# Two steps of expert tiles a round instead of three in the last rounds of a transformer kernel

## The reference

```python
x = x + _L0_xattn_ref(ctx_1024, _layernorm(x), mask, ...)     # 8 heads, keys from context and tokens
x = x + _L0_ffn_ref(_layernorm(x), weight_q, weight_scale, bias)   # int8 quantised 128x128 product
x = x + _L1_xattn_ref(_layernorm(x), ctx_1024, We, W2)        # softmax over the tokens
x = x + _L1_ffn_ref(_layernorm(x), Wr, br, W1, b1, W2, b2)    # 8 experts, argmax router
```

## Time and profile before

| | us |
|---|---|
| median of 3 runs | 1051.12 |
| lowest and highest | 1049.69, 1051.59 |
| the profiled execution | 1048.07 |
| its span in the trace | 1046.3 |
| mean granted TensorE clock in it | 0.986 |
| TensorE busy | 979.4 |
| VectorE busy | 795.1 |
| ScalarE busy | 740.3 |
| GpSimd busy | 468.0 |

### The profile page before, as it was taken

One profiled execution on the slowest core, in us unless ns is written; L12 is line 12 of the kernel. 1 busy time (PEld: TensorE's weight loads), 2 busy tenths in 40 slices (PEclk: granted clock), 3 DMA queues, 4 the chain that ended last, 5 costly groups with the idle time before them and its releaser, 6 DMA issues.

```text
span 1046.3 us, 31979 instructions
## 1 busy us (share of the span) xinstructions
PE 979.4 (94%) x10989; PEld 861.2 (82%) x10989; DVE 795.1 (76%) x2585; ACT 740.3 (71%) x1753; POOL 468.0 (45%) x1094
## 2 busy tenths in 40 slices
PE   2799999999999999999999999999998988887997
PEld 1688888888888888888888888888887878877897
DVE  3566778888888888888888888888888867755553
ACT  1688877777777777777777877777776655554564
POOL 3333323353545353535353535343434335664455
PEclk9999999999999999999999999999999998998999
DMA  5743000000000000000000000000000032011310
GB/s 133 213 115 61 3 2 2 2 12 2 12 1 10 0 10 0 10 0 10 0 10 0 10 3 8 3 7 5 5 7 6 5 70 74 30 34 50 87 50 22
DMA packets 45124, 28.38 MB, mean 27 GB/s; under 512 B 11039, under 2 KB 41698, under 8 KB 45042
## 3 DMA queue, kind: packets, MB, share of 16 engines
q1 hardware_dynamic: 39586, 17.79, 6.8%
q0 software_dynamic: 4320, 8.50, 2.5%
q10 hardware_dynamic: 1136, 1.05, 0.3%
HBM read 17.75 MB, written 10.02 MB: 27 GB/s over the span
## 4 chain that ended last, share of the span: by engine, by line
PE 80%; ACT 5%; DVE 4%; issue 4%; SPq 3%; POOL 2%; another core or an unknown queue 1%; DMA 1%; DVEq 0%; POOLq 0%; ACTq 0%
PE ps L1421 13%; PE ps L1384 10%; PE ps L1362 8%; PE ps L1188 7%; PE ps L1190 7%; PE ps L1189 7%; PE ps L1460 7%; PE ps L1349 4%; PE ps L1341 4%; PE ps L1446 3%; PE ps L1440 2%; SPq L399 2%; SPq L400 1%; PE ps L1216 1%; PE ps L1231 1%
## 5 line engine op out<-in xcount | busy, mean ns | idle before, releaser
L1080 DVE TENSOR_REDUCE sumsq<-qk_hat 128x8 f32<-128x512 f32 x192 | 124.0, 678 | 44.9 <-ACT qk_hat L491 44.6
L1421 PE MATMUL ps<-qT_all,kT_all 64*128 64x128 f32 x2048 | 149.6, 286 | 1.8 <-ACT w_all L500 1.2
L1384 PE MATMUL ps<-v_sb,prob 128*64 128x65 f32 x4096 | 144.5, 224 | 6.2 <-ACT qq_t L541 2.4
L1384 PEld LDWEIGHTS ps<-v_sb,prob 128*64 128x64 f32 x4096 | 129.0, 138 | 25.3 <-issue 13.3
L550 ACT ACTIVATE prob<-ps,neg_shift 128x512 f32<-128x512 f32 x128 | 88.6, 692 | 79.4 <-PE ps L1421 79.3
L1103 DVE TENSOR_TENSOR qk_hat<-ps,rstd 128x512 f32<-128x512 f32 x192 | 120.6, 684 | 26.9 <-POOL rstd L686 26.3
L491 ACT ACTIVATE qk_hat<-ps 128x512 f32<-128x512 f32 x192 | 113.3, 598 | 39.1 <-PE ps L1190 28.9
L1421 PEld LDWEIGHTS ps<-qT_all,kT_all 64*128 64x128 f32 x2048 | 125.0, 188 | 19.2 <-ACT prob L550 13.1
L1188 PE MATMUL ps<-w_hi,xc_hi 128*128 128x512 f32 x320 | 138.3, 432 | 0.8 <-DVE mask_bias L1155 0.8
L679 POOL TENSOR_TENSOR rs_t<-rs_y 128x32 f32<-128x32 f32 x73 | 17.8, 243 | 259.7 <-ACT rs_y L528 259.7
L1190 PE MATMUL ps<-w_hi,xc_lo 128*128 128x512 f32 x320 | 126.6, 396 | 0.0
(11 more groups left out here) (227 smaller groups left out, 2142.1 us busy)
## 6 DMA issues: line engine op xcount, KB each, us to landing
x_res<-sorted_rows SPq DMA_DIRECT2D x71, 65.5 KB
w_all<-in_L_ffn_W_dram SPq DMA_DIRECT2D x16, 256.0 KB, 5.9
x_res<-in_x_dram SPq DMA_DIRECT2D x5, 768.0 KB
ctx_res<-in_ctx_dram SPq DMA_DIRECT2D x5, 462.0 KB
out_dram<-o_n,x_res POOLq DMA_INDIRECT x71
sorted_rows<-stage,idx POOLq DMA_INDIRECT x64
sorted_rows<-fill SPq DMA_DIRECT2D x1, 524.0 KB, 5.2
sorted_rows<-table_fill SPq DMA_DIRECT2D x8, 65.5 KB
```

The source lines that it names most:

```text
L1080: nc.vector.reduce_sum(sumsq[:, n * H:(n + 1) * H], sq[:, n * INNER:(n + 1) * INNER].rearrange("p (h d) -> p h d", d=DH), AX).then_inc(ss_ ...
L1384: last = nc.tensor.matmul(dst[half:half + DH, :], prob[:, kt, at + half:at + half + DH], v_sb[:, 1 - par, kt, h, :], start=kt == 0, stop=k ...
L1421: last = nc.tensor.matmul(ps_s[2 * kt + half][:, cols], k_t[rows, kt, cols], q_t[rows, cols], start=True, stop=True)
```

## The change

Each of the rounds 64 to 74 takes two steps instead of three. The calls of place 1 go away on TensorE, ScalarE, VectorE and GpSimd; those of places 0 and 2 stay where they are in the order and take consecutive tiles. `tile_no` numbers them by `place // 2`. `REST`, the loop over the first list behind the last round, starts at step 21 instead of 32, so that 20 tiles of that list have their first product there, where it was 9. The table of the second list is still built in its first four steps. Number and order of the tiles, arithmetic and buffers are the same.

```diff
--- before.py
+++ after.py
@@ -327,7 +327,7 @@
         def one(res, b):
             return res[:, bass.ds(b, 1), 0:D].rearrange("p a d -> p (a d)")
 
-        TAIL, PLACES = B, 3
+        TAIL, PLACES = B, 2
         TOTAL_AT = 4 * (EARLY + 2) + 3
 
         def tail(j, inside):
@@ -335,7 +335,7 @@
 
         def tile_no(j, place):
 
-            return PLACES * (j - TAIL) + place - 1
+            return PLACES * (j - TAIL) + place // 2 - 1
 
         REST = range(PLACES * (LAST + 1 - TAIL) - 1, NA + 1)
         SECOND_PART = range(NA - 2, T + 1)
@@ -529,7 +529,6 @@
                                              bias=lift_bias[:, 0:1]).then_inc(y0_done, 1)
 
                 if tail(j, inside):
-                    tile(tile_no(j, 1), 0)
                     roots()
                 if rho == 0 and group(g - 1, inside):
 
@@ -703,7 +702,6 @@
                     nc.gpsimd.tensor_copy(mask_now[:, 1 - par:2 - par], mask_bias[:, bass.ds(j + 1, 1)]).then_inc(mask_set, 1)
 
                 if tail(j, inside):
-                    store(tile_no(j, 1), 0)
                     if g - 2 == NG - 1 and rho == 0:
                         scatter(g - 2, (0, 1), inside)
                     store(tile_no(j, 2), 0)
@@ -1065,10 +1063,8 @@
                 window(j, par, rho, g, inside)
                 if tail(j, inside):
                     finish(tile_no(j, 0), 0)
-                    prep(tile_no(j, 1), 0)
                     if rho != 0:
                         later(j, par, rho, g, inside)
-                    finish(tile_no(j, 1), 0)
                     prep(tile_no(j, 2), 0)
                     if rho == 0:
                         later(j, par, rho, g, inside)
@@ -1373,8 +1369,6 @@
                         last = product(ps_v[kt], xc_hi[:, par, kt, :], xc_lo[:, par, kt, :], 2 * INNER)
                         last.then_inc(v_done, 1)
                 slot_b(j, rho, g, inside)
-                if tail(j, inside):
-                    tile(tile_no(j, 1), 0)
                 def weighted(heads):
                     for h in heads:
                         dst = ps[:, 3 if h < H // 2 else 4, h % (H // 2) * VW:(h % (H // 2) + 1) * VW]
```

## The result

The changed kernel takes 1060.24 us (median of 4, 1059.56 to 1060.95) beside 1050.92 for the kernel before on the same chip (4 executions, 1049.69 to 1051.59). The ratio is 1.009 [1.0075, 1.0105]: slower, by 9.3 us. The forecast was 1053.6, slower by 2.5, with 1060.0 as the range's end. So the side was right, and the size was not; the value lies 0.24 us outside the range. The right side is weak evidence: 1053.6 stood 0.4 us over the border to "same", and "slower" had a chance of 0.45.

The account below looks back on a forecast made before the run. TensorE alone was taken to bound the part behind the rounds, the engines' chain most rounds. Rounds -12.4, later part +20.9, seam -5.0, stall -1.0 gave +2.5 us: median 1051.12 to 1053.6, range 1044.5 to 1060.

Parts of the forecast that it names:

- what bounds the later part: Behind the last round TensorE alone binds; 11 moved steps at 1.90 us each cost +20.9 us.
- the chain is a floor in most rounds: Rounds 64 to 74: the chain of quantised layer, attention and router limits what they give back, -12.4 us in sum.
- Two more signs that the prediction named: TensorE waits in rounds 66, 68, 73 for ScalarE's or GpSimd's work, not tile rows; regular 1.90 us from about step 26.
- round 64: First edited round: a 0.55 us wait and a product of about 1 us ahead of the last attention heads, -1.7 us.
- rival A: Idle stretches in rounds 65, 66, 68 and 73 slow following steps through the clock: +6.4 us, 1060, chance 0.18.
- the argument against A: In most of the idle stretches in the rounds TensorE is early, so slow matmuls are absorbed.
- A's own sign: Granted clock of rounds 66 to 74 under 0.85 would show the clock rival.
- the seam, -5.0: Between the two lists: TensorE's gap from late row loads closes as the row is needed later; -5.0 us, bounds 0 and -5.0.
- Rival C: The change doesn't do what it says; only a seam stall that stays remains of this case: 1058.6, chance 0.05.
- the stall, -1.0: First steps behind the rounds: about 8 us lost there, ScalarE standing 4.78; -1.0 us taken, bounds 0 and -8.
- the prediction's own test: ScalarE stall over 4 us about 6 us behind the rounds means the phase makes it; at step 33, the instruction stream.
- uncovered: VectorE's table steps behind the rounds, about 4 us over four steps, would cost about 2 us if not covered.

Follow-up runs that it names:

- the two plain runs: The changed kernel as it is, run twice more on other chips: 1051.69 beside 1040.75 (ratio 1.0117) and 1052.97 beside 1040.21 (ratio 1.0135).
- e2_after_one_list: The changed kernel with both lists of tiles run as one pipeline behind the rounds: 1047.21 beside 1040.49, ratio 1.0074.
- e4_after_pad_later: The changed kernel with the padding rows issued later, after the 27th final sum: 1054.78 beside 1040.49, ratio 1.0139.
- r5_after_again: The changed kernel once more, as it is, on another chip: 1051.69 beside 1040.75, ratio 1.0117.
- e3_before_one_list: The kernel before with both lists of tiles run as one pipeline: 1037.39 beside 1040.49, ratio 0.9959.
- e7_two_in_65_69: The kernel before with two steps only in rounds 65 to 69, three in 64 and 70 to 74: 1046.01, ratio 1.0053.
- e10_before_one_list_busy: The kernel before with one pipeline for both lists and filler transposes in waits of rounds 65 and 73: 1034.4 beside 1040.21, ratio 0.9954.
- e3_again: The kernel before with one pipeline for both lists, repeated on another chip: 1043.45 beside 1046.92, ratio 0.9964.

## Why the prediction was right and wrong

**Right: what bounds the later part.** +20.13 us from the count to tile 40, where the prediction had 20.9 - 1.0 = 19.9. Each moved step costs its 1.90.

**Right: the chain is a floor in most rounds.** In the pair, round by round from 64: +1.6, -0.8, 0.0, -3.5, +1.3, +0.4, -0.2, -2.9, -0.8 (72 and 73 up to the matmul of the centred rows) and -2.8. The forecast was -1.7, 0, 0, -3.3, 0, -0.6, -1.1, -2.3, -1.8, -1.6. Rounds 67 and 71 gave what was walked out, 65, 66 and 68 gave nothing, and GpSimd's 7.9 us stayed. One pair is noisy by 1 us in a round. The mean of five traces with two steps (the pair's, the two plain runs, `e2_after_one_list` and `e4_after_pad_later`) less that of three with three steps (the pair's and the two of one list) is +0.5, -0.6, +0.3, -3.8, +0.1, -0.5, -0.4, -2.7, -1.4, -1.6: -10.0 in sum, and within 0.7 of each term but the first. The kernels that change only rounds 65 to 69 or 70 to 74 agree with the terms to 0.4 us in their medians. Two more signs that the prediction named are there: in rounds 66, 68 and 73 TensorE waits for ScalarE's copies (3.05 and 1.01 us) and GpSimd's centred rows (2.77 us), and the regular pace begins at step 26.

**Wrong in size: round 64.** The prediction put -1.7 there, from the 0.55 us wait and the product that leave the path. It gave +1.6 in the pair and +0.5 in the mean. The steps removed were counted and the idle time that they leave was not: TensorE stands 1.92 us where the step stood, and what follows runs in part at 1.2 GHz, which 14 transposes without use prevent. The size is less sure than the cause: the round takes 13.7 to 15.25 us in six traces with two steps and 13.6 to 14.7 in seven with three, three of which have the low clock there too. This is rival A's mechanism, but in a round that the rival didn't name; its list was 65, 66, 68 and 73. In those, slow matmuls were absorbed, as the argument against A said: raising the clock there brought nothing that can be measured. A's own sign didn't come either: over rounds 66 to 74 the granted clock is 0.88 (0.93 before), not under 0.85.

**The step that failed: the seam, -5.0.** It gave -0.7. The gap was put down to rows that come late, since the loads are issued from 966.84 and the row is prepared at 978.09. The program's own order has the gap whatever the loads do, and `SECOND_PART = range(NA - 2, T + 1)` says so: it restarts a pipeline that `REST` had drained. The earlier trace rows held the hint: VectorE had idled only 0.43 us ahead of that row. One pipeline over both lists closes the gap in the changed kernel, and in the kernel before all of it or all but 0.9 us. The 0.7 that did come is not a later load but the clock: the window 973.70 to 986.30 had 0.86 before, and the seam has 1.00 after. In the plain run `r5_after_again` it is 0.88, and the five steps take 14.5 us, as in the kernel before. Rival C had this outcome, 1058.6, at a chance of 0.05.

**Wrong by little: the stall, -1.0.** From the count at 942.15 to the regular pace at 957.48 the changed kernel needs 15.3 us for some four steps (7.6), so 7.7 go there, as about 8 did. By the prediction's own test the phase behind the rounds makes it and not the instruction stream: the stall, 3.88 us, ended 6 us behind the rounds, and none stood at step 33. But in both kernels it came in the second step of the loop, 22 and 33, so the place in the loop and the time since the rounds aren't told apart. What makes ScalarE stand is open. Of the time lost, 3 to 3.5 us can be VectorE's table work, as on the chips without the stall. The 2 us that the prediction gave it "uncovered" were too little.

**Not foreseen: +1.3 us behind the seam.** 0.35 goes with step 56, which is long in both (3.25 us after, 2.76 before); 0.9 comes after the last product. Both are taken up in the last section.

With the measured terms the sum is -10.0 + 20.9 + 0 (seam, within 0.7) + 0 (stall) + 0.9 = +11.8, for medians of +9.3, +10.9 and +12.8. The range ended too low since the sum's own spread held 4 us for the rounds and nothing for the seam, although the seam's paragraph gave 0 as a bound; in the pair the rounds missed by 4.7 us and the seam by 4.3.

## What to carry to other kernels

Where a consumer waits between two loops, first read whether the loops' ranges drain and refill a software pipeline; only then look at the loads, and ask how long the releaser itself had waited. Filler work pays for its place in the chain with the engine's clock as well: take it out only where the engine is early anyway, and cost the work right behind the hole at the slow rate. Moving work from a stretch with waits to one that is saturated costs its full busy time there, so what it must give back is to be summed wait by wait.

## What the runs showed of the hardware

**The clock in round 64.** The granted clock of the window 844 to 858 was 0.75 to 0.88 in the six traces with two steps in round 64 and no filler, 0.96 to 1.00 in the three with filler, and 0.88 to 1.00 in the seven with three steps. So filler kept the clock up, but the hole of 1.92 us isn't needed for the fall: in three of the seven with three steps (`e3_before_one_list`, `e7_two_in_65_69`, `e10_before_one_list_busy`, 0.88 each) the clock fell 3.4 to 3.9 us into the round, behind no idle time longer than 1.3 us. The Trainium skill, "TensorE: Matmul & The Clock Gate", Part 1, says that activity releases the clock; the runs agree, and the activity here was transposes by matmul.

**ScalarE's stalls belong to a chip, and one to a place.** On the pair's chip and on the one with 1046.9 ScalarE stands 3.9 to 4.8 us behind the rounds. None of the 13 traces from the other four chips has an idle time of ScalarE that ends by the unnamed queue from round 64 on. On the same two chips the time from the transpose of tile 55 to that of tile 56 (step 56 above) is 2.8 to 3.6 us, and 1.90 on the others. ScalarE there, kernel after:

```profile
1018.93 0.28 ACT L449 ACTIVATE xc_t<-ps 128x128 f32<-128x128 f32 x1 [1.60 <-remote]
```

The kernel before with one list, on the chip with 1046.9:

```profile
1002.28 0.28 ACT L449 ACTIVATE xc_t<-ps 128x128 f32<-128x128 f32 x1 [1.90 <-remote]
```

They are 16 us apart in time, and both are the copy of tile 55. So this one is bound to a place in the program. The first came at step 22 after and at step 33 before and in `e3_again`. What either waits for isn't shown. The chips differ elsewhere too: the eight padding writes are issued over 12.03 to 12.35 us where ScalarE stalls and over 8.1 to 8.3 us on the others.

**The end grows with the steps that are moved.** The last product on TensorE, kernel after:

```profile
1051.11 1.15 PE L1345 MATMUL ps<-w_all,kT_all 128*128 x8 [0.43 <-issue]
```

Up to the end of the span it is 8.1 us, and 7.2 in the kernel before (1039.12 to 1046.3), with the same last stores. It is 7.1 to 7.2 in all four traces with three steps in every round, 7.6 in the two with five steps moved, 8.0 with ten, and 8.1 in all with eleven: about 0.08 us for each step moved, on every chip. The trace shows where it lies: in GpSimd's closing `DRAIN`, which begins 2.15 us behind that product in all of them and ends the span. Kernel before and kernel after:

```profile
L67 POOLq DRAIN  x1: 4797/4797/4797, 1041.3 to 1041.3; - x1
```

```profile
L67 POOLq DRAIN  x1: 5692/5692/5692, 1053.3 to 1053.3; - x1
```

It is 5.20 us with five steps moved and 5.62 with ten. Why it grows, with the same number of scatters ahead of it, isn't shown.
